# One queue of loads in a new order: the held context's fetch moves early, the next context's load moves last

## What is computed

```python
x = x + tanh(g_xattn[0]) * L0_xattn(layernorm(x), ctx)        # 4 heads, softmax over 375 keys
x = x + tanh(g_ffn[0])   * (linear + low-rank delta)(layernorm(x))
x = x + tanh(g_xattn[1]) * L1_xattn(layernorm(x), ctx, ctx)   # one head, softmax over 375 keys
x = x + tanh(g_ffn[1])   * (attention of 16 heads over the 112 rows + mixture of 8 experts, top 2)
```

## Time and profile before

| what | value |
|---|---|
| median of 3 runs (lowest, highest) | 911.13 us (910.73, 918.67) |
| the profiled execution: time, and its span in the trace | 918.06 us, 916.3 us |
| mean granted TensorE clock over the span | 0.971 |
| busy share: PE, PEld, DVE, ACT, POOL | 90%, 72%, 77%, 59%, 51% |
| moved by DMA | 63.31 MB, mean 69 GB/s |

### The profile page before, as it was taken

The page is one execution under the profiler, slowest core; times in us unless marked ns, Lnnn a source line. Parts: engine busy times, 40 slices in busy tenths (PEclk is TensorE's granted clock), DMA queues, the critical chain, the costliest instruction groups (busy, mean ns, idle before and its releaser), DMA issues. The chain is left out here.

```text
span 916.3 us, 33626 instructions
## 1 busy us (share of the span) xinstructions
PE 820.2 (90%) x11440; PEld 657.1 (72%) x11440; DVE 703.2 (77%) x1647; ACT 541.8 (59%) x1232; POOL 471.7 (51%) x748
## 2 busy tenths in 40 slices
PE   3578999999989999999999999999999999999875
PEld 2457777777777778777777787777777877877754
DVE  1677788778777778878887788888777888888653
ACT  2354666655666665666666656666666566666443
POOL 6722554454554455455545554555455555645454
PEclk9779999999999999999999999999999999999898
DMA  9222221122221122222211222221112222221100
GB/s 326 89 74 72 78 60 51 45 76 76 76 75 34 43 76 76 76 76 71 61 49 47 76 76 76 76 71 59 44 53 76 76 76 76 64 62 44 38 7 11
DMA packets 40966, 63.31 MB, mean 69 GB/s; under 512 B 5292, under 2 KB 27204, under 8 KB 40676
## 3 DMA queue, kind: packets, MB, share of 16 engines
q1 hardware_dynamic: 40932, 62.87, 22.9%
HBM read 49.96 MB, written 12.89 MB: 69 GB/s over the span
## 5 line engine op out<-in xcount | busy, mean ns | idle before, releaser
L1199 POOL TENSOR_SCALAR ln_ve<-ln_mv 112x1 f32<-112x1 f32 x128 | 81.8, 639 | 214.4 <-DVE ln_mv L944 214.4
L1309 POOL TENSOR_TENSOR part<-part 112x256 f32<-112x256 f32 x224 | 165.7, 740 | 20.9 <-ACT part L817 6.0
L817 ACT ACTIVATE part<-bankE,cgS 112x256 f32<-112x256 f32 x256 | 107.2, 474 | 26.9 <-POOL cgS L1289 22.0
L329 PE MATMUL bankE<-wexs_hi,xT_hi 128*112 128x512 f16 x256 | 101.9, 398 | 15.5 <-ACT part L817 15.1
L329 PE MATMUL bankE<-wexs_hi,xT_lo 128*112 128x512 f16 x256 | 98.5, 385 | 0.0
L329 PE MATMUL bankE<-wexs_lo,xT_hi 128*112 128x512 f16 x256 | 98.5, 385 | 0.0
L1203 POOL TENSOR_TENSOR ln_rs<-ln_ve,cst 112x1 f32<-112x1 f32 x128 | 89.8, 702 | 10.7
L1272 POOL TENSOR_SCALAR pick<-cst,topf,top 112x8 f32<-112x8 f32 x32 | 13.2, 413 | 156.4 <-DVE topf L1075 156.4
L1087 DVE TENSOR_REDUCE mx<-quad 112x8 f32<-112x896 f32 x64 | 69.5, 1086 | 7.3 <-PE quad L557 4.4
L1045 DVE TENSOR_TENSOR p_lo<-p2T,p_hi 112x896 f16<-112x896 f32 x64 | 68.5, 1070 | 6.1 <-ACT p_hi L802 6.1
L966 DVE TENSOR_REDUCE mx<-quad 112x2 f32<-112x750 f32 x64 | 57.1, 936 | 6.6 <-PE quad L424 6.6
(11 more groups left out here) (229 smaller groups left out, 3185.6 us busy)
## 6 DMA issues: line engine op xcount, KB each, us to landing
ctf<-in_ctx_T SPq DMA_DIRECT2D x32, 375.0 KB, 3.1
ctn<-in_ctx_n SPq DMA_DIRECT2D x32, 375.0 KB
hold<-kvA SPq DMA_DIRECT2D x32, 281.2 KB, 7.0
kc<-hold SPq DMA_DIRECT2D x32, 187.5 KB
xin<-in_x SPq DMA_DIRECT2D x32, 112.0 KB, 2.0
x<-in_x SPq DMA_DIRECT2D x32, 112.0 KB, 6.6
out_x<-xout SPq DMA_DIRECT2D x32, 112.0 KB, 1.9
wex<-in_w_exp SPq DMA_DIRECT2D x1, 2048.0 KB, 10.2
```

What stands on the lines that cost most here:

```text
L329: last = mm(o, w, m, start=(n == 0), stop=(n == len(terms) - 1))
L817: act.activation(part[:, e, :], bankE[0:LQ, n * D:(n + 1) * D], ACT.Identity, scale=cgS[:, e:e + 1])\
L1199: pool.tensor_scalar(ln_ve[n][:], ln_mv[n][:, 1:2], EPS, None, ALU.add).then_inc(ln[n].sem, 1)
L1309: pool.tensor_tensor(part[:, k, :], part[:, k, :], part[:, k - 1, :] if k else x3[:], ALU.add).then_inc(moe_sum[j].sem, 1)
```

## The change

Only SP's body is written in another order. Before, in an iteration: load x(a), load the next context (a+1), load the untransposed context (c), write a's context to `hold`, load x again for the residual (b), fetch the held context (c), store (e). After: load x(a), store (f), fetch the held context (c), load x for the residual (b), load the untransposed context (c), write a's context to `hold`, load the next context (a+1). The functions and their waits are unchanged, and so are all other engines. The store is of f and not of e, that is the same output, issued from the next iteration's body.

```diff
                 if A and not first(a): load_x(a)
                 if A: load_weights(a)
-                if A and more: load_ctx_T(a + 1)
+                if FF: store(f)
+                if C: fetch_held(c)
+                if B: load_x0(b)
                 if C: load_ctx_n(c)
                 if A: hold_context(a)
-                if B: load_x0(b)
-                if C: fetch_held(c)
-                if EE: store(e)
+                if A and more: load_ctx_T(a + 1)
```

## The result

The change makes the kernel faster: 879.19 us median (878.87 to 880.77, 4 runs) against 911.02 (4 runs), a ratio of 0.9635 with a 95% interval of 0.9583 to 0.9686. The profiled execution took 879.08 us, its span 877.3. Predicted were 879.0, and 872 to 892 as the range.

What follows compares the result with a forecast made beforehand. PE, the busiest engine, stalls at scores1 for kcm: 918.06 us profiled less 35.4 (stalls) and 2.8 (clock) is 879.9; from the 911.13 median, without stalls, 878.4. Predicted 879.0, range 872 to 892.

Steps and rivals of the forecast that it cites:

- What bounds the kernel: PE waits at scores1 for kcm, 37.0 us in 28 stalls; each adds to a rigid 25.10 us iteration.
- The fetch in time: Issued at scores1_T's end, kcm lands by 422, some 10 us before the next scores1; the loop's 27 stalls go.
- Why it was late: In SP's queue the fetch waits 12.6 us behind the wait for kvA's low parts; kcm lands 4.6 us after issue.
- The rule weighed: Skill's transfer price, about 2.0 us fixed plus bytes over 436 GB/s, set aside for the 4.6 us from kcm's issue.
- The second rival: At scores1, an event other than kcm ends the wait, so the change does nothing: 911 us, 903 to 918; chance 0.06.
- The residual at `qp_lo`: scores1 also needs qp_lo, so 0.02 us of each stall stays, 0.5 us over 27 stalls.
- The other engines: DVE, ACT and POOL idle longer than the 1.17 us PE gains, so they follow; smallest margin DVE's, 0.33 us.
- the rival: DVE or a transfer's landing becomes the new wait; half a microsecond per iteration back gives 893 us; chance 0.08.
- The clock: Two falls of the granted clock to 0.50 in the loop, after long stalls, vanish: 1.4 us each, 2.8 saved.
- The sum: Savings on the profiled execution: 35.4 us from stalls plus 2.8 from the clock, 38.2 together, giving 879.9 us.
- the first stall: PE's 1.20 us wait at 65.68 while the pipeline fills; 0.1 us saved, bounds 0 and 1.2.
- The other loads: SP's x for the residual, ctn and hold move earlier, ctf later; no cost, ctf keeping 4 us at worst.

Runs made afterwards that it cites:

- e3: Kernel before, with the store of e and the fetch exchanged, so the fetch goes out behind the store: 1046.07 us, ratio 1.1455.
- e10: Kernel before, with only the load of the untransposed context (ctn) moved ahead of the next context's load: 877.04 us, ratio 0.9609.
- e13: Kernel before, order untouched, with ctn padded from 125 to 128 rows: 876.90 us, ratio 0.9618.
- e8: Changed kernel, with three more statistics instructions on DVE ahead of the row maximum of scores1: 899.16 us, ratio 0.9856.
- e14: Kernel before, with an extra 375 KB transfer of 125 partitions directly ahead of the fetch: 1045.54 us, ratio 1.1449.
- e12: Kernel before, with an extra 375 KB transfer of 128 partitions directly ahead of the fetch: 944.13 us, and 959.03 us when run again.
- e1: Kernel before, with only the fetch moved early, directly behind the load of x(a): 877.55 us, ratio 0.9612.
- e9: Changed kernel, with DVE's three gate steps put ahead of the layer-0 residual x1: 871.41 us, ratio 0.9558.
- e2: Changed kernel, with only the fetch put back, behind all other transfers: 879.70 us, ratio 0.9621.
- e5: Changed kernel, with the next context's load put off into the next iteration, directly behind the store: 882.69 us, ratio 0.9663.
- e11: Kernel before, with an extra 512-byte transfer directly ahead of the fetch: 912.40 us, ratio 0.9978.

## Why the prediction was right, point by point

**What bounds the kernel.** The stall at `scores1` holds the whole loop: confirmed. It is gone, the distance is 25.10, and it grows by the stall and more in e3. PE is busy for 24.74 of 25.10 us.

**The fetch in time.** Right. It was to go out at the end of `scores1_T`, 3.8 us behind the start of `scores1`, and it goes out 4.0 behind it (393.19 against 389.23).

**Why it was late.** The prediction said: SP reaches it late, behind a foreign condition, and it lands 4.6 us behind its issue. Both are so, but the second was taken as given, as the price of a landing, and 3 us of it were queueing. That is where the cause lies. With the fetch still behind that condition, the stall vanishes when `ctn` goes ahead (e10) or has 128 rows (e13). A fetch in the same burst with an evenly spread `ctn` is in time. The 125-row transfer ahead of it made it late; that the late position left it no room for this is the prediction's own sum. The account was half of the mechanism, and the time came out right because the change removes both halves: with the fetch first, neither the condition nor `ctn` is ahead of it. So far it was luck, since the half that the prediction didn't see is enough by itself (e10, e13). No run has an early fetch behind a `ctn` of 125 rows, so that the other half is enough too is argued from the room of 10 us and not shown.

**The rule weighed.** I set the 2.0 us of the Trainium skill (DMA: Bandwidth & Descriptors, Anatomy of one DMA) aside since a burst took 4.6. The lone fetch took 1.5 (e3), so the page's order of size was right and the difference was queueing. The rule on the number of transfer engines, which the Trainium skill states further down that page (Why a DMA increments its semaphore by 16 and not by 1), points at `ctn` before any run. The second rival, that the change does nothing, falls in any case.

**The residual at `qp_lo`**, 0.02 us of each stall: the loop runs at 25.10 to 25.11 where that step gave 25.12. It is 0.4 us in all.

**The other engines.** DVE's margin was predicted as 0.33 and is 0.33. e8 made the rival real, and showed a margin nearer to 0.4.

**The clock.** Right: no fall in the loop after, 2.8 us back. The runs with long stalls, e3 and e14, have a fall in every iteration of the loop, behind PE's standing for 4.0 to 5.6 us; e12, with stalls around 2.2, has three in all outside fill and drain.

**The sum.** Between `scores1` number 1 and number 29, before: 803.15 - 65.68 = 737.47; after: 765.80 - 66.97 = 698.83; 38.6 us less, where the sum gave 35.8 - 0.5 + 2.8 = 38.1. The drain is shorter by 1.6 (before 916.3 - 803.15 = 113.15, after 877.3 - 765.80 = 111.5). Against that the first `scores1` comes 1.3 later: PE's first layer-1 product, whose inputs both kernels load in the same order before the change begins, starts at 18.48 instead of 16.33. Half of that was there before the first reordered issue: POOL began to prepare one input at 15.44 instead of 14.34, and SP's new order begins at 16.30. Whether the exchange of `hold` and `ctf` has a share in the rest is open, and nothing speaks for it: the first `scores1` is at 64.8, 65.8, 66.2 and 68.4 in e13, e10, e1 and e3, which keep the old order of the two, and at 65.2, 66.5 and 67.0 in e9, e2 and the changed kernel, which have the new one. It moves by as much within one order as between the two. Of the first stall 0.2 went, where 0.1 was taken: PE still waits 1.02 there instead of 1.20, for `qp_lo`. The errors of the three parts cancel to 879.08 against 879.9 for the profiled execution, and that the median, 879.19, came so near to 879.0 is luck.

**The other loads.** No cost, as predicted; `ctf` has more room than it needs (e5).

## What to carry to other kernels

A wait for a transfer has two ends, when it is issued and what is ahead of it in the transfer engines. Before reordering a queue, look at the shape of the transfers ahead: one of 125 partitions held up what stood behind it three times as long as the same bytes in 128, and padding it was worth as much as the new order. And when a stall sits on the engine that bounds a loop, subtract it and look at once for the smallest idle behind it on the other engines: that is how far the gain goes.

## What the runs showed of the hardware

384,000 bytes ahead of a fetch lengthened the stall by 0.96 us with 128 partitions (e12) and by 2.92 us with 125 (e14). A transfer of 125 partitions alone in the transfer engines kept them busy to a share of 0.32, at 129 GB/s. A 512-byte transfer and its issue slot lengthened it by nothing measurable (1.24 against 1.32 us, e11). A lone fetch of five transfers was there 1.50 us behind its last issue (e3). At every stall of 4.0 to 5.6 us in the loops of e3 and e14 the granted clock fell to 0.50, mostly for 3.4 us, and an iteration was then 1.2 us (e3) to 1.5 us (e14) longer than the stall explains.
